# Last batch of an expert layer: the second matrix product in two passes by halves of the output width

## The reference, cut to what matters

```
grouped = x.reshape(b, s // 32, 32, d)                     # 32 groups of 32 tokens
logits  = einsum('bntd,des->bntes', grouped, Wc) + bc      # 32 x 4 = 128 experts
perm    = (logits == max over the 32 tokens)               # each expert takes one token of a group
permuted = einsum('bntd,bntes->bnesd', grouped, perm)
inner    = relu(einsum('bnesd,esdf->bnesf', permuted, W1) + b1)   # 512 -> 32
result_p = einsum('bnesf,esdf->bnesd', inner, W2) + b2            # 32 -> 512, "second layer"
result   = einsum('bnesd,bntes->bntd', result_p, perm)            # back to the tokens
x = x + tanh(g_ffn) * result
```

## Time and profile before

| | us |
|---|---|
| median of three executions | 1761.32 |
| lowest, highest | 1755.34, 1763.64 |
| the profiled execution's own time | 1774.67 |
| its span, first to last instruction | 1772.9 |

### The profile page before, as it was taken

The page is one execution under the profiler, slowest core; times in us unless marked ns, Lnnn a source line. Parts: engine busy times, 40 slices in busy tenths (PEclk is TensorE's granted clock), DMA queues, the critical chain, the costliest instruction groups (busy, mean ns, idle before and its releaser), DMA issues.

```text
span 1772.9 us, 51861 instructions
## 1 busy us (share of the span) xinstructions
PE 1638.3 (92%) x22488; PEld 1147.6 (65%) x22488; DVE 1296.2 (73%) x1886; ACT 736.4 (42%) x965; POOL 854.9 (48%) x1016
## 2 busy tenths in 40 slices
PE   7899999999999999999878999999988989998995
PEld 4677777777777777777656555666555666554663
DVE  5677777787777777777717777677777777776866
ACT  3532323233332333233234555454555554555552
POOL 3368777877778777877611222122222122222122
PEclk9999999999999999999989999999999999999997
DMA  7634545554454545454554887777888777878765
GB/s 273 171 98 148 172 142 176 156 164 159 148 189 159 167 145 177 155 165 148 185 188 141 214 216 212 210 204 201 223 212 213 214 209 198 208 204 226 213 170 157
DMA packets 180882, 324.81 MB, mean 183 GB/s; under 512 B 23344, under 2 KB 33328, under 8 KB 179248
## 3 DMA queue, kind: packets, MB, share of 16 engines
q1 hardware_dynamic: 135728, 239.68, 42.5%
q0 software_dynamic: 17280, 31.46, 11.0%
q10 hardware_dynamic: 27648, 50.34, 8.9%
HBM read 242.71 MB, written 78.71 MB: 181 GB/s over the span
## 4 chain that ended last, share of the span: by engine, by line
PE 57%; DMA 19%; DVE 12%; issue 5%; ACT 3%; POOL 2%; SPq 1%; ACTq 0%; POOLq 0%; DVEq 0%
PE ps L1435 12%; PE ps L899 10%; PE ps L946 10%; DMA xin<-out 7%; PE ps L1408 6%; DMA out<-xin 5%; PE ps L959 5%; PE ps L914 3%; PE ps L972 3%; DVE mx L694 2%; DMA gat<-in_W 2%; PE ps L1459 2%; DMA sel<-lg_scratch 2%; PE ps L933 2%; ACT lg L663 2%
## 5 line engine op out<-in xcount | busy, mean ns | idle before, releaser
L182 POOL TENSOR_SCALAR xin<-xin,r_all,nb_all 128x512 f32<-128x512 f32 x128 | 112.2, 880 | 524.7 <-DMA xin<-out 377.4
L1339 DVE STREAM_TRANSPOSE res<-res 128x2048 f32<-128x2048 f32 x128 | 292.1, 2295 | 0.1
L1289 ACT ACTIVATE gat<-ps 128x1536 f32<-128x1536 f32 (+1 forms) x128 | 170.9, 1344 | 235.4 <-PE ps L1408 235.2
L1355 DVE COPY res<-ps 128x1024 f32<-128x1024 f32 x128 | 156.7, 1225 | 85.3 <-PE ps L1459 66.2
L899 PE MATMUL ps<-xTh,qh 128*128 128x512 f32 x512 | 209.5, 409 | 5.0 <-DVE qs L711 1.4
L1408 PE MATMUL ps<-sel,xin 32*128 32x128 f32 x4096 | 157.2, 284 | 51.0 <-issue 25.7
L899 PE MATMUL ps<-xTh,ql 128*128 128x512 f32 x512 | 200.8, 392 | 0.0
L899 PE MATMUL ps<-xTl,qh 128*128 128x512 f32 x512 | 200.3, 391 | 0.0
L1345 DVE COPY gat<-ps 128x512 f32<-128x512 f32 (+1 forms) x128 | 104.1, 816 | 102.6 <-PE ps L1408 102.4
L1408 PEld LDWEIGHTS ps<-sel,xin 32*128 32x128 f32 x4096 | 131.9, 186 | 65.5 <-issue 38.9
L1299 ACT ACTIVATE res<-ps 128x1024 f32<-128x1024 f32 x128 | 131.0, 1024 | 101.0 <-PE ps L1459 90.4
(11 more groups left out here) (156 smaller groups left out, 3335.2 us busy)
## 6 DMA issues: line engine op xcount, KB each, us to landing
gat<-in_W ACTq DMA_DIRECT2D x192, 256.0 KB, 5.1
xT<-in_xT SPq DMA_DIRECT2D x32, 1024.0 KB, 6.2
xin<-in_x SPq DMA_DIRECT2D x64, 512.0 KB, 3.8
out<-xin SPq DMA_DIRECT2D x64, 512.0 KB, 4.3
xin<-out SPq DMA_DIRECT2D x128, 256.0 KB, 4.1
xin<-in_W SPq DMA_DIRECT2D x128, 256.0 KB, 3.9
out<-xin POOLq DMA_DIRECT2D x120, 256.0 KB, 7.5
xT<-in_W SPq DMA_DIRECT2D x68, 256.0 KB, 4.6
```

What stands on the lines that cost most here:

```text
L182: e.tensor_scalar(self.xn[:, t, :], self.xn[:, t, :], self.r[:, i, t:t + 1], self.nb[:, i, t:t + 1], ALU.mult, ALU.add).then_inc(self.m_xn ...
L1289: e.activation(o, v, ACT.Copy).then_inc(m_gaA.sem, 1)
L1339: e.transpose(v, v).then_inc(m_tr.sem, 1)
L1355: e.tensor_copy(o, v).then_inc(m_evV.sem, 1)
```

## The change

In the last batch the second layer is no longer eight steps of full width. It is 16 steps `outer_last(n)` of half the width: n = 0..7 make columns 0 to 255 for u = 0..7, n = 8..15 columns 256 to 511 for u = 0..7 once more. The copies of the first pass are shared by ACT and DVE as before, at half the size; those of the second pass are both made by ACT. DVE goes from its eight half copies straight to `swap` 0 to 3, and to `swap` 4 to 7 when ACT's copies of the second pass are done. The other 15 batches are not touched.

```
+            for n in range(16):                                  # scalar
+                for jp in range(2 if n >= 8 else 1):
+                    e.wait_ge(m_w2.sem, of_last(m_w2, n))
+                    o, v = half_pair(n % 8, jp, n // 8)
+                    e.activation(o, v, ACT.Copy).then_inc(m_evA.sem, 1)
...
             def swap(i, k):                                      # vector
-                if k == 0:
+                if i == B - 1 and k % 4 == 0:
+                    half_copied(e, 7 if k == 0 else 14)
+                    half_copied(e, 7 if k == 0 else 15)
+                elif k == 0:
                     copied(e, i, 7)
...
-                    if live(i):
+                    if live(i) and i < B - 1:
                         rest(i, u)
+                    elif live(i):
+                        e.wait_ge(m_w2.sem, of_last(m_w2, u))
+                        o, v = half_pair(u, 1, 0)
+                        e.tensor_copy(o, v).then_inc(m_evV.sem, 1)
...
+            def outer_last(n):                                   # tensor
+                u, w = n % 8, slice(n // 8 * 2 * P, (n // 8 + 1) * 2 * P)
+                if u in W2_MOVED:
+                    e.wait_ge(d_room[u].sem, d_room[u].at(B - 1, d_room[u].per - 1))
+                if n >= 2:
+                    half_copied(e, n - 2)
+                elif n == 0:
+                    e.wait_ge(m_hr.sem, m_hr.at(B - 1, 7))
+                else:
+                    finished(e, B - 2, NT - 1)
+                for j in range(4):
+                    r = slice(j * F, (j + 1) * F)
+                    e.matmul(ps[:, bank(u) + j, w], rowk[r, u // 2, :], b2s[r, u % 2, w],
+                             start=True, stop=False, skip_group_check=True)
+                for k in range(4):
+                    for j in range(4):
+                        r = slice(j * F, (j + 1) * F)
+                        last = e.matmul(ps[k * NG:(k + 1) * NG, bank(u) + j, w], hid(B - 1)[r, 8 * k + u, :], second(B - 1, u)[r, k, w],
+                                        start=False, stop=True, skip_group_check=True)
+                last.then_inc(m_w2.sem, 1)
...
             def scatter_last(k):
+                if k % 2 == 0:
+                    half_copied(e, 14 + k // 2)
                 e.wait_ge(m_tr.sem, m_tr.at(B - 1, 2 * k + 1))
```

More of the change, by code:

```diff
@@ L1101, in experts @@
         m_finV = mark("finV", 2)
+        of_last = lambda m, k: m.at(B - 1 + k // 8, k % 8)
         m_xn, m_sel = route.m_xn, route.m_sel
@@ L1168, in copied, with half_pair, half_copied @@
             e.wait_ge(m_evV.sem, m_evV.at(i, u))
+        def half_pair(u, jp, w):
+            o, v = pair_of(u, jp)
+            return (o[:, w * P:(w + 1) * P], v[:, w * P:(w + 1) * P])
+        def half_copied(e, n):
+            if n < 8:
+                e.wait_ge(m_evA.sem, of_last(m_evA, n))
+                e.wait_ge(m_evV.sem, of_last(m_evV, n))
+            else:
+                e.wait_ge(m_evA.sem, of_last(m_evA, 2 * n - 7))
         def finish(e, i, t):
@@ L1461, in outer @@
                 last.then_inc(m_w2.sem, 1)
+            def outer_last(n):
[6 more added lines that the diff above has]
+                    e.wait_ge(m_hr.sem, m_hr.at(B - 1, 7))
+                else:
+                    finished(e, B - 2, NT - 1)
[9 more added lines that the diff above has]
+                last.then_inc(m_w2.sem, 1)
             def scatter(i, t):
@@ L1506, in tensor @@
                 for u in range(8):
-                    if live(i):
+                    if live(i) and i < B - 1:
                         outer(i, u)
+                for n in range(16):
+                    if i == B - 1:
+                        outer_last(n)
                 for h in range(2):
```

## The result

The change made the kernel slower: a median of 1773.21 us (1768.98 to 1778.24, 11 executions) against 1762.63 for the kernel before in the same rounds, ratio 1.0075 [1.0048, 1.0101]. The medians are 10.6 us apart; the ratio alone would make it 13.2 (8.5 to 17.8 by its interval). A second series of the same kernel gave 1.0056 [1.0036, 1.0075]. The forecast was no change: 1761.0, with a range of 1755 to 1766.

What follows compares the result with a forecast made beforehand. The prediction took chain B, DMAs and POOL's adds, to bound the end, with all added work hidden: span 1772.9 + 0.0. No change from 1761.3, given as 1761.0 for a small chance of gain; range 1755 to 1766.

Steps and rivals of the forecast that it cites:

- 8 more bias groups and 8 more groups of 16 matmuls: Last batch's second layer on PE: the added half-width matmuls were to be hidden in PE's 6 us of idle time.
- A half step of pass 1: First pass of the last batch: a half-width step on PE was to take 0.9 us, between bounds 0.75 and 1.50.
- Step 7 starts: First pass's last step: ready at 1733.6, it was to wait for the last W2 quarter, landing at 1736.19.
- From step 7 to the first scatter: Second pass: ACT's sixteen copies of 0.60 us were to set the pace, 1.25 a step; first scatter at about 1747.1.
- the point from which this decides: First scatter must end by 1753.4, start by 1749.8 at 3.64 us; ACT's copies decide from 0.82 us each.
- rival 2: Second pass: ACT's 16 copies alone become the bound, making every chain B add up to 3.3 us late, 1764.6; chance 0.04.
- Rival 4: Pass 1 ends so late that transposes 0 to 3 don't lie beside pass 2; no gain, 1761.3; chance 0.03.
- Rival 3: Transposes hold up POOL's third and fourth result issues, making chain B 2.2 to 4.4 us later; chance 0.05.
- Rival 1: Chain A's gain reaches the kernel's end: up to 2.0 us, at most 3.4, giving 1759.3 or 1757.9; chance 0.08.
- chain A: The work the change moves: DVE's copies, eight transposes, scatters, final DVE operation; ended 2.08 us before the third adds.
- chain B: The bounding waits: W2 landing, POOL's result issues, attention read-back, POOL's adds, ACT's gated copy, SP's stores; forecast unchanged.
- an active second pass would keep PE's clock up: PE at work until the scatters was to give the higher clock, scatters of 1.96 us and chain A's end at 1760.8.

Runs made afterwards that it cites:

- filler: The changed kernel with three idle full-width matmuls put ahead of step 5 of the first pass: 1775.24 us, ratio 1.0072 to the kernel before.
- pad_front: The kernel before with 576 more PE instructions, as 144 tiny 8x8 matmuls at the very start ahead of the attention: ratio 1.0071.
- pad_idle16: The kernel before with 16 groups of 8-column matmuls (1152 PE instructions) added ahead of the last batch's scatters: ratio 1.0123.
- before_early: The kernel before without POOL's wait for the last quarter of W2 in the last batch, so batch 14's results go out earlier: 1760.54 us, ratio 0.9987.
- pad_pe: The kernel before with eight groups of 8-column matmuls (576 PE instructions) appended at the very end: ratio 1.0050.
- after_again: The changed kernel once more, unchanged, against the kernel before: ratio 1.0056.
- pad_idle8: The kernel before with eight groups of 8-column matmuls (576 PE instructions) in PE's idle time ahead of the last batch's scatters: ratio 1.0043, repeated 1.0065.
- halves_in_step: The kernel before with each last-batch step's matmuls issued as two halves of 256 columns, same order, copies and transposes: 1777.88 us, ratio 1.0083.

## Why the prediction was wrong

**The step that failed** is the one that priced the added matmuls: "8 more bias groups and 8 more groups of 16 matmuls, of half width, hidden in the 6 us that PE sat idle". I counted PE's time by the width of the matmuls and never asked whether it can be fed them at that pace. The standstills, put at nothing, measured 0.66 and 2.43 us in the first pass, and PE's part of a step of the second pass, put at 0.9 us, measured 1.61 at 1.2 GHz. The page's part on DMA queues lists a queue of kind "instruction":

```profile
q8 instruction: 181, 2.97, 0.7%
```

That is 2.97 MB in 181 packets, 16 KB each; before had 179. I take a packet to bring one block of 256 instructions, since about 128 matmuls with their loads lie between standstills (126 to 128 by the records, of which some are missing).

The Trainium skill's page "Runtime: NRT & Kernel Launch" (section "Instruction fetch mechanics") gives the same size of a block, and says that crossing a block is mostly hidden. The trace agrees with the size; that it is hidden holds here only where a block lasts long enough.

The packets' times in the traces, found by asking for ever narrower windows, show that PE waits for them. In after they start at 1722.23 and 1728.32, and PE goes on at 1724.43 and 1730.56, 2.20 and 2.24 us later. A look at 1728.2 to 1728.4:

```profile
q8 instruction: 1, 0.02, 27.9%
```

The 20 profiles mark 710 standstills of over 0.2 us behind 900 us. In the middle half of them PE went on 2.27 to 2.43 us after a packet had started. No experiment changed the fetch alone, but the count of 128, the moves of the standstills in filler and pad_front, and these times leave little else.

How long PE stands depends on two things. One is how fast it uses a block up. A full step is 36 matmuls in 1.50 us, so a block lasts 128/36 x 1.50 = 5.3 us; at half width PE used one in 3.70 us (1724.43 to 1728.13). The other, which no experiment set out to vary, is how soon the next packet starts, and that goes with the load of the DMA engines. From PE's going on after a standstill to the next packet's start it took 1.1 us where the DMA engines were busy for under 0.1 of that time (median of 226 cases), and 3.5 us where it was over 0.9 (58 cases). In after, at a share of 0.86, it was 3.89 us; with the 2.24 behind it that makes 6.13 for a block that lasted 3.70, and the difference is the 2.43 of standstill. pad_idle16 has the same narrow matmuls behind four standstills. Its windows from PE's going on to the next packet (the last two numbers are DMA share and GB/s):

```profile
1740.51:1742.84 2.33, 2.06 (x128) 1.84 (x128) 2.33 (x2) 0.00 (x0) 0.00 (x0) 0.57 0.98 180
1745.08:1748.47 3.39, 2.66 (x128) 2.39 (x128) 3.39 (x3) 0.00 (x0) 0.00 (x0) 0.50 0.86 301
1750.74:1751.80 1.06, 1.06 (x60) 0.99 (x60) 1.06 (x1) 0.00 (x0) 0.00 (x0) 0.50 0.05 15
1754.21:1755.32 1.11, 1.11 (x72) 1.05 (x72) 0.68 (x1) 0.00 (x0) 0.00 (x0) 0.50 0.00 0
```

The standstills that followed the first three took 2.50, 3.00 and 1.29 us. Full width, with 5.3 us a block, is not safe either. In the last layer of seven of the twelve kernels that have it at full width no step is late, but with the same matmuls one was late by 0.2 us in before, 0.8 in pad_idle16, 1.0 in pad_front and 1.1 in pad_pe (the row below took 2.31 where its neighbours took 1.14), and two by 1.2 and 1.4 in before_early, whose results went out at that time.

```profile
1727.93 2.31 PE L1459 MATMUL ps<-gat 32*32 32x512 f32 x32
```

The trace of before already held the warning, in a view I hadn't asked for: the groups of PE from 915 to 1700 us, with the idle time before them and what ended it.

```profile
L1408 PE MATMUL ps<-sel,xin 32*128 32x128 f32 x3711 | 142.7, 284 | 47.6 <-issue 23.5 <-ACT sel L213 12.7 <-POOL xin L182 9.6
```

The gather's narrow matmuls lose 23.5 us to "issue". This loss is no part of the difference: after has 20.1 there.

**What followed, by the steps of the prediction** (times from the layer's start, forecast against measured):

- A half step of pass 1: 0.9 against 0.97 to 1.03. Right.
- Step 7 starts: 8.9 (the landing of W2) against 11.6. The landing came at about the forecast time, before 1728.46 by POOL's row, or 8.7; it was PE's standstill that made step 7 late, 2.7 us beyond the forecast. The first transpose came at 14.2 instead of 10.9.
- From step 7 to the first scatter: 10.9 against 14.8 (1731.40 to 1746.24). Nine steps at 1.61 instead of ACT's 1.25 make 3.2 of the 3.9. The pace was set by PE at 1.2 GHz, not by ACT: its copies were released by PE every time.
- The first scatter therefore starts at 26.4 instead of 19.8. The prediction put the point from which this decides at an end by 1753.4, or 26.1 after the start. It ended at 29.2 (1749.00), 3.1 too late; the tail grew by 3.2. In after_again it ended 30.2 after the start, and the tail grew by 4.2.

So rival 2's place and price (3.3 us) came true by another engine, which is luck. Its own condition, ACT's copy above 0.82 us, did not: the copy took 0.60, as forecast. Rival 4 was false: transposes 0 to 3 did lie beside the second pass. Rival 3 stays untested: POOL's issues ran from 1728.46 to 1731.98, before the first transpose at 1734.02. Its ground was also misread. The longest issue, 1901 ns, is the fourth of the burst: the four took 0.86, 1.20, 1.55 and 1.90 us in before and the same in after, where DVE was idle until 1731.44. So no row shows that another engine can hold an issue up. The third and fourth of before started at 1737.62 and 1738.16, not at 1738.3. Rival 1's gain could not come, since chain A became late; but chain A and chain B do lie within some 2 us of each other. In pad_front, whose last batch is that of before, the chain of waits ended through the transposes and DVE's last operation, with a tail of 43.5.

I also argued that an active second pass would keep PE's clock up. The row says otherwise: 0.51 for 15.6 us in which PE was never idle. In the first scatter it was 0.70, and the last two scatters took 1.96 us each, as at the higher level. I had cited the Trainium skill's page "TensorE: Matmul & The Clock Gate" (section "What's actually happening"), by which activity releases the throttle; the scatters fit that, the second pass doesn't.

**The other 6.4 to 7.4 us** (10.6 less the 3.2 and 4.2 of the two profiles) lie ahead of the tail, which "the change touches nothing before 1727 us" excluded. This remainder is known only roughly: the interval of the total is 9 us wide, and the tail of untouched last batches varies from 43.5 to 45.6. It arises in the expert layer, between the first batch and the last: the first batch's second layer starts at 914.0 to 916.8 whether the program is longer or not, pad_front aside.

That it comes with the number of PE instructions, wherever these stand, is shown by pad_pe, the two runs of pad_idle8 and pad_front. pad_pe's 0.50% is 8.8 us, and 47.7 - 45.4 = 2.3 of it is tail (45.4 is the mean of before and its two copies), where the pads themselves run until 1762.36 of a span of 1765.8. By the same sum, an estimate from ratio and tail, 5.1 and 9.5 us of the two runs of pad_idle8 are not tail.

Why it is so stays open. It is not shown to be proportional: 1152 gave 9.4 us ahead of the tail by that sum, no more than 576. It is not a shift of the blocks against the program, since pad_pe and pad_idle8 leave all earlier instructions where they were. It is not the standstills in the gather (18 to 25 us in every kernel with the biases but pad_front, with no order by length), nor all of PE's standstills from 915 to 1700 us (31 to 38 us in the six profiles with up to 72 more, 31 to 39 in the ten with about 576, both 34 to 35 in the mean). The duration of the DMAs didn't tell the kernels apart either. One possibility that wasn't tried is where the program and the tensors lie in memory.

No version that gives the full result beat the kernel before: 0.9987 [0.9961, 1.0013] for before_early is no difference.

## What to carry to other kernels

Splitting matmuls costs instructions even where it costs no columns. Ahead of such a change, ask the trace of before for PE's idle time that "issue" ended. Then work out how long a block of 128 matmuls lasts at the planned pace, and compare it with what the next packet needs. By the medians here that is an estimate of 1.1 + 2.3 = 3.4 us where the DMA engines are idle and 3.5 + 2.3 = 5.8 us where they are busy. Where the block is shorter, expect PE to stand for the difference, and price what follows at the lower clock too, until rows say otherwise. And where a total has to be explained to 0.5%, time a program that only has as many more instructions in a place where they do nothing, before looking for the cause in the code.

## What the runs showed of the hardware that was not expected

- PE stood still for 0.2 to 4.1 us without any releaser, about every 128 matmuls or a multiple of that: in half-width steps (a block in 3.7 us) and in the gather (about 4.2 us), and at full width (5.3 us) in five of twelve kernels, by 0.2 to 1.4 us in a step. It goes on some 2.3 us after a packet of queue q8 has started, and that packet starts later the busier the DMA engines are (1.1 us against 3.5).
- After a standstill of 2.43 us the granted clock was 0.51 for 15.6 us of matmuls of half width back to back; matmuls of full width on the same 32x32 tiles held 1.00 in all of the earlier trace rows's first stretch. In all six kernels with the biases and half-width steps the clock fell around a standstill of 1.2 to 2.7 us: from 0.7 us before PE went on (after_again) to 2.3 us after (halves_in_step). Standstills of 0.4 to 0.7 us ahead of those didn't bring it down. In filler it came back after 6.8 us, with half-width steps still running (0.50 from 1742.5 to 1749.3, 1.00 from 1749.4 to 1750.5), so the width alone doesn't decide. What does is open.
- A PE program longer by 576 instructions makes the kernel 0.43 to 0.71% longer. With them at the end or in the last batch's idle time, 5 to 10 us of that arise ahead of the place where they stand; one longer by 72 costs nothing measurable. The cause is open.
